# A three-layer graph kernel: the loads of the column numbers move from SyncE's DMA queue to ScalarE's

## The reference

```python
def _spmm(row, col, vals, x):
    msg = vals[:, None] * x[col]
    return jax.ops.segment_sum(msg, row, num_segments=N)

def _layer(x_prev, row, col, vals, W_a, b_a, W_b, b_b):
    h = _spmm(row, col, vals, x_prev)
    z = (h + x_prev) @ W_a.T + b_a + h * x_prev @ W_b.T + b_b
    return jnp.where(z >= 0, z, NEG_SLOPE * z)
```

## Time and profile before

| | |
|---|---|
| median of three runs | 11672.61 us (11668.24 to 11686.65) |
| the profiled execution | 11676.03 us |
| its span in the profile | 11674.3 us |
| TensorE busy | 9811.1 us (84%) |
| VectorE busy | 8287.8 us (71%) |
| ScalarE busy | 3867.5 us (33%) |
| three expansions, TensorE's first to last instruction of each | from 4527, 6908 and 9291 us, for 875, 872 and 877 us in the windows |
| DMA over the span | 1744.93 MB, mean 149 GB/s; in the expansions 335 to 337 GB/s |

### The profile page before, as it was taken

One profiled execution on the slowest core, in us unless ns is written; L12 is line 12 of the kernel. 1 busy time (PEld: TensorE's weight loads), 2 busy tenths in 40 slices (PEclk: granted clock), 3 DMA queues, 4 the chain that ended last, 5 costly groups with the idle time before them and its releaser, 6 DMA issues.

```text
span 11674.3 us, 234500 instructions
## 1 busy us (share of the span) xinstructions
PE 9811.1 (84%) x66108; PEld 8442.8 (72%) x66109; DVE 8287.8 (71%) x13757; ACT 3867.5 (33%) x12047; POOL 5876.3 (50%) x4395
## 2 busy tenths in 40 slices
PE   6898997689999947998888789988787899878877
PEld 4677776467777736997676679986666799867666
DVE  6877776777777746776666667766666677766666
ACT  0566665046666602662000036630000256400001
POOL 7577776047777710003777710027777300177774
PEclk8666666766666657999999999999999999999999
DMA  2111111011111194998666779986666799966666
GB/s 78 17 4 4 4 4 15 5 3 4 4 4 4 4 26 158 343 341 256 190 191 187 184 190 343 346 275 190 186 190 187 158 338 346 303 187 192 190 188 139
DMA packets 1150180, 1744.93 MB, mean 149 GB/s; under 512 B 472915, under 2 KB 524183, under 8 KB 1149494
## 3 DMA queue, kind: packets, MB, share of 16 engines
q0 software_dynamic: 430880, 809.77, 30.8%
q1 hardware_dynamic: 719254, 934.66, 27.1%
HBM read 990.83 MB, written 752.96 MB: 149 GB/s over the span
## 4 chain that ended last, share of the span: by engine, by line
DMA 24%; issue 17%; PE 15%; DVE 3%; POOL 2%; ACT 2%; POOLq 1%; SPq 0%; DVEq 0%; ACTq 0%
DMA messages<-work 13%; DMA work<-messages,work 11%; PE ps L885 6%; PE ps L876 6%; POOL work L499 2%; ACT work L658 2%; DVE work L1248 2%; PE ps L856 2%; PE ps L893 1%; PE ps L913 1%; PE ps L914 1%; POOLq L497 0%; PE ps L903 0%; SPq L576 0%; POOLq L493 0%
## 5 line engine op out<-in xcount | busy, mean ns | idle before, releaser
L499 POOL DMA_INDIRECT work<-messages,work x3000 | 3250.7, 1084 | 4194.6 <-issue 4022.7
L885 PE MATMUL ps<-work 128*128 128x125 f32 x24000 | 3394.6, 288 | 910.4 <-DVE work L1248 878.4
L885 PEld LDWEIGHTS ps<-work 128*128 128x128 f32 x24000 | 2911.5, 193 | 1393.5 <-DVE work L1248 1379.8
L475 POOL DMA_INDIRECT sorted_edges<-stage,run_idx x1270 | 2420.2, 1906 | 1456.4 <-DMA sorted_edges<-stage,run_idx 535.4
L1248 DVE SCALAR_TENSOR_TENSOR work<-work,iota_p 128x500 f32<-128x500 f32 x3000 | 2219.9, 740 | 1295.7 <-DMA work<-messages,work 1281.3
L876 PE MATMUL ps<-xb,work 125*128 x21504 | 2458.0, 276 | 149.7 <-DVE work L1220 83.0
L876 PEld LDWEIGHTS ps<-xb,work 125*128 125x128 f32 x21504 | 2423.7, 192 | 183.9 <-issue 183.5
L769 PEld LDWEIGHTS ps<-hT 128*128 128x128 f32 x12700 | 2187.4, 272 | 392.5 <-issue 371.4
L769 PE MATMUL ps<-hT 128*128 128x80 f32 x12700 | 2190.7, 357 | 286.6 <-ACT hT L617 217.7
L658 ACT ACTIVATE work<-ps,work 128x128 f32<-128x128 f32 x5376 | 1511.4, 371 | 1394.1 <-PE ps L876 730.7
L614 ACT ACTIVATE hT<-iota_p,place 128x128 f32<-128x128 f32 x4826 | 1437.2, 387 | 403.4 <-DVE place L1057 381.1
(11 more groups left out here) (199 smaller groups left out, 3843.1 us busy)
## 6 DMA issues: line engine op xcount, KB each, us to landing
messages<-work SPq DMA_DIRECT2D x2688, 256.0 KB, 6.2
work<-slot_cols SPq DMA_DIRECT2D x672, 256.0 KB, 6.0
work<-messages,work POOLq DMA_INDIRECT x3000, 3.8
sorted_edges<-stage,run_idx POOLq DMA_INDIRECT x1270, 3.2
out_x<-xb SPq DMA_DIRECT2D x150, 125.0 KB
work<-lane_places SPq DMA_DIRECT2D x508, 5.5 KB, 3.4
out_x<-xb SPq DMA_DIRECT2D x4, 1562.5 KB
sorted_edges<-hT SPq DMA_DIRECT2D x4, 906.0 KB
```

The costliest lines, as they stand in the source:

```text
L475: pool.indirect_dma_start(out=sorted_edges[p], out_offset=bass.IndirectOffsetOnAxis(ap=run_idx[:, q, k:k + 1], axis=0), in_=stage[:, q, k ...
L499: pool.indirect_dma_start(out=ck[:, n, :], out_offset=None, in_=messages, in_offset=bass.IndirectOffsetOnAxis(ap=idx[:, h * BU + n:h * BU ...
L885: last = t.matmul(part[n], ck[:, n, j * D:(j + 1) * D], sel[:, n % SELB, j, :], start=j == 0, stop=j == CH - 1)
```

## The change

SyncE no longer issues the loads of column numbers. ScalarE does: the first four of a layer ahead of its first body, and in each body one load after each of the messages 2, 6, 10 and 14, for the same buffer of the next body, after a wait for the four one-hots that read the buffer. ScalarE's bodies are written as first, middle and last, since the last body loads nothing; SyncE's are now all alike. The wait for `cols_stored` (the table is in HBM) moves along.

```diff
--- before.py
+++ after.py
@@ -562,27 +562,15 @@
             sp.dma_start(row_at, tile_rows.rearrange("p t -> (p t)")[0:TB].rearrange("(a t) -> a t", a=1)).then_inc(offsets_in, DMA)
             sp.dma_start(base_of, tile_base.rearrange("p t -> (p t)")[0:TB].rearrange("(a t) -> a t", a=1).to_broadcast([P, TB])).then_inc(offsets_in, DMA)
             sp.dma_start(messages[0:CHUNKS, CH * D:REC].rearrange("(p c) j -> p c j", p=DP), slot_row).then_inc(slots_stored, DMA)
-            sp.wait_ge(cols_stored, DMA)
-
-            cols_of = slot_cols.rearrange("(n c) -> n c", c=BATCH * GE)
             new_out = out.rearrange("(n h r) (l d) -> n l r h d", h=2, r=BLK, d=D)
             with sp.Fori(0, LAYERS) as la:
-                def load_cols(i, h):
-                    sp.dma_start(col_row[:, h, :], cols_of[bass.ds(i * CB + h, 1), :].to_broadcast([P, BATCH * GE])).then_inc(col_row_in[h], DMA)
-
-                def store_messages(i, last):
+                def store_messages(i):
                     for n in range(AU):
                         sp.wait_ge(msg_ready[n % 2], la * (GROUPS // 2) + i * (AU // 2) + (ACREDIT + n // 2 + 1))
                         sp.dma_start(messages[bass.ds(i * (AU * P) + n * P, P), 0:CH * D], msg[:, n % MR, :]).then_inc(msg_stored[n % MR], DMA)
-                        if n % BATCH == BATCH - 1 and not last:
-                            sp.wait_ge(col_hot_ready, la * GROUPS + i * AU + (n + 1))
-                            load_cols(i + 1, n // BATCH)
-
-                for h in range(CB):
-                    load_cols(0, h)
-                with sp.Fori(0, ABODIES - 1) as i:
-                    store_messages(i, False)
-                store_messages(ABODIES - 1, True)
+                with sp.Fori(0, ABODIES) as i:
+                    store_messages(i)
+
                 with sp.Fori(0, DSTEPS // DU) as i:
                     for k in range(DU):
                         sp.wait_ge(xb_ready, la * DSTEPS + i * DU + (k + 2))
@@ -638,6 +626,8 @@
                 s.activation(val_of.rearrange("p (t k j) -> p k j t", k=GPP, j=CH)[:, k, :, :],
                              ps[:, k, 0:CH * DP].rearrange("p (j t) -> p j t", j=CH), ACT.Copy).then_inc(vals_kept, 1)
             act.wait_ge(vals_kept, GPP)
+            act.wait_ge(cols_stored, DMA)
+            cols_of = slot_cols.rearrange("(n c) -> n c", c=BATCH * GE)
 
             with act.Fori(0, LAYERS) as la:
                 def free_message(eng, i, n, first):
@@ -647,7 +637,10 @@
                     elif not first:
                         eng.wait_ge(msg_stored[n % MR], la * (GROUPS // MR * DMA) + i * (AU // MR * DMA))
 
-                def keep_messages(i, first):
+                def load_cols(i, h):
+                    act.dma_start(col_row[:, h, :], cols_of[bass.ds(i * CB + h, 1), :].to_broadcast([P, BATCH * GE])).then_inc(col_row_in[h], DMA)
+
+                def keep_messages(i, first, last_body):
                     act.wait_ge(msg_ready[0], la * (GROUPS // 2) + i * (AU // 2) + ACREDIT)
                     s.activation(val_now, val_of[:, bass.ds(i * (AU * CH), AU * CH)], ACT.Copy).then_inc(val_now_ready, 1)
                     act.wait_ge(val_now_ready, la * ABODIES + i + 1)
@@ -658,10 +651,17 @@
                             last = s.activation(msg[:, n % MR, j * D:(j + 1) * D], ps[:, n % PR, j * D:(j + 1) * D], ACT.Copy,
                                                 scale=val_now[:, n * CH + j:n * CH + j + 1])
                         last.then_inc(msg_ready[0], 1)
-
-                keep_messages(0, True)
-                with act.Fori(1, ABODIES) as i:
-                    keep_messages(i, False)
+                        if n % BATCH == BATCH - 2 and not last_body:
+                            act.wait_ge(col_hot_ready, la * GROUPS + i * AU + (n + 2))
+                            load_cols(i + 1, n // BATCH)
+
+                for h in range(CB):
+                    load_cols(0, h)
+                keep_messages(0, True, False)
+                with act.Fori(1, ABODIES - 1) as i:
+                    keep_messages(i, False, False)
+                keep_messages(ABODIES - 1, False, True)
+                act.sem_inc(act_copies, 1)
 
                 with act.Fori(0, BBODIES // 2) as i:
                     for h in range(2):
```

## The result

The changed kernel takes 11777.77 us, median of 4 runs (11759.19 to 11782.69), beside 11679.63 us for the kernel before in the same comparison (11668.24 to 11694.44). The ratio is 1.008, 95% interval [1.0067, 1.0094]: slower by 98 us. The forecast was 11636 us, 37 us less than the 11672.61 us measured for the kernel before at that time. The profiled span is 11776.1 us, 101.8 us longer than before.

What follows compares the result with a forecast made beforehand. The prediction took DMA rate, through free message buffers and VectorE, to bound the expansions. From 11676.0 us it took 36 (transfers) and 2 (layer starts), then 3.4 for the median, and said 11636 us; range for 8 in 10: 11575 to 11725.

Steps and rivals of the forecast that it cites:

- what bounds the kernel: In the three expansions: DMA rate sets when message buffers are free, then VectorE's scaling, its one-hot and TensorE's gap.
- the gap between bodies: TensorE's idle time between expansion bodies, 0.77 us of 15.35 us each, set by how far VectorE is ahead.
- the issue on ScalarE: Four load issues a body, 0.36 us each, hidden in ScalarE's idle time: 0, at most 7 us slower.
- The start of a layer: First four loads go out about 1 us earlier at two of three layers: 2 us gained.
- the transfers: Loads in another queue overlap stores, recovering a quarter of their surplus: 0.22 us a body, 36 us gained.
- a load's surplus: A load's extra DMA time over a store, estimated at 0.94 less 0.724 us from the mixed and last-body windows.
- a worse mix: Rival side of the transfers: the 0.22 us added once more per load, 145 us slower; 0.05 with a late ScalarE.
- a late ScalarE: Rival: ScalarE issues of 1.5 us or more exceed its idle cover twice a body; 0.05 with a worse mix.
- that place is what goes away: On SyncE's queue, the load's place between store 3 and store 4 of its quartet disappears; no time was given.
- an inner rate over 350 GB/s: Sign that the forecast is right: DMA rate in the inner stretch of an expansion.
- The overtaking: Rival: loads in their own queue delay store 3 by 0.38 us a body, 63 us slower, 11736 us; chance 0.23.
- Its signs: For the overtaking: loads landing under 5 us, stores over 6.3 us, VectorE's store waits over 85 us in 700.

Runs made afterwards that it cites:

- e16: Kernel before with the loads of column numbers in the bodies left out; 11607.15 us, ratio 0.99, 117 us faster.
- e7: Kernel before, loads still on SyncE's queue but behind the stores of messages 1, 5, 9 and 13; 11817.35 us, ratio 1.0088.
- e10: Kernel before, loads still on SyncE's queue but behind the stores of messages 2, 6, 10 and 14; 11794.72 us, ratio 1.0084.
- e3: Kernel before with the loads issued by GpSimd in a queue of its own, once the four one-hots are made; 12240.75 us, ratio 1.0036.
- e9: Changed kernel with each ScalarE load held until odd message 3, 7, 11 or 15 is made; 11745.5 us, ratio 1.0049 to the kernel before.
- e13: Kernel before, on SyncE, only a body's first load moved, from behind store 3 to behind store 1; 11753.29 us, ratio 1.0025.
- e6: Changed kernel, unchanged, run again on another chip; 11833.98 us, ratio 1.01 to the kernel before.
- e5: Kernel before, unchanged, run again for a profile beside the other runs; 11698.63 us in a single run.
- e14: Kernel before, on SyncE, first load left behind store 3, the others moved behind stores 5, 9 and 13; 11732.66 us, ratio 1.0007.
- e1: Kernel before with TensorE's read of 16 offsets done once a layer instead of once a body; 12181.17 us, ratio 0.9992.
- e2: Changed kernel with TensorE's read of 16 offsets done once a layer; 12253.71 us, ratio 1.0047 to the kernel before.
- e4: Kernel before with TensorE's read of 16 offsets moved behind group 0, into the body's work; 13134.33 us, ratio 1.0773.
- e17: Kernel before, on SyncE, loads behind the stores of messages 1, 7, 11 and 13; 12263.65 us, ratio 1.0032.
- e18: Kernel before, on SyncE, loads behind the stores of messages 1, 5, 9 and 15; 12322.16 us, ratio 1.0075.

## Why the prediction was wrong

**Right: what bounds the kernel.** The expansions, the full DMA engines and the gap between bodies were the place: 97.5 of 101.8 us. e16 confirms that DMA rate and gap hang together and what lies in them.

**Right: the issue on ScalarE.** 0.34 us against 0.36 taken; ScalarE is no later for it, since it waits longer for TensorE than before. The start of a layer brought nothing measurable: outside the expansions the trace differs by 4 us, the other way.

**The step that failed: the transfers.** The prediction took a quarter of a load's surplus of 0.22 us over a store as recovered, -36 us. The term measured +97.5 us, 0.59 us for each of 165 bodies (worked out). It had named the other side, a worse mix at up to 145 us more, but gave it, together with a late ScalarE, a chance of 0.05. Two things stood in it without a price. The first is the place: "that place is what goes away" is said in the part on what the change removes, and no term follows. e7 and e10 lose 0.88% and 0.84% with one queue and with SyncE issuing everything, and in e7 the first load of a body ends 0.83 us behind the store ahead of it instead of 0.38, so what a load costs depends on the order around it. The second is the other queue, taken as a gain: e3, with the loads in their old order among the stores, loses 0.36%, and e9, with the loads back at about their old places, 0.49%. The change does both at once and loses 0.8 to 1.0%. Either alone costs, the place alone as much as the whole; how the loss of this kernel divides between them is not shown.

**A reading that was not quite right.** The earlier trace rows are called free of loads, but the last load was issued at 5377.9 us and landed at 5383.9 (worked out). A stretch behind it:

```profile
5384.00:5390.00 6.00, 6.00 (x56) 6.00 (x55) 4.39 (x10) 3.98 (x15) 0.00 (x0) 1.00 1.03 366
```

By 366 GB/s a load's surplus comes to 0.26 us instead of 0.22. That is not what failed.

**The test was misread in advance.** The prediction held that an inner rate over 350 GB/s would show it right. It came to 330 at a share of 1.04. A DMA share above 1 was read as engines that can't be slower, only better mixed; it says how long packets were under way, and packets can take longer.

**The rival that came nearest.** The overtaking was priced at 11736 us and put its finger on store 3 and the gap between bodies; the measured time is 42 us above it and outside the range. e10 fits its place: one step ahead of store 3, the whole loss. Its signs did not come, so its nearness in time says nothing for its mechanism. Loads of a queue of their own did not land in under 5 us but in 5.7, stores at 6.2 rather than over 6.3, and VectorE waits 67 us for stores, not over 85. By the rule of the Trainium skill (page "DMA: Bandwidth & Descriptors", section "Queues, rings and completion order") that queues take turns, the load should have been served ahead of some of the stores queued before it. The landing times, of the first engine or of the last, don't show that. And overtaking isn't needed: a single queue, with no second one to take turns with, loses as much. A load ahead of store 3 in every body, which the rival priced at 63 us, costs 29 us on one queue (e13). By the same page of the Trainium skill, section "Issuing engines are not separate DMA queues", the time would not have changed. Nothing was gained, as it says, but the measured time rose, and e3 loses 0.36% with the order kept.

**What stays open.** Why a load two places earlier is served slower. In the slow kernels fewer transfers are under way when the first load goes out: 5.8 to 6.8 in e6, e7 and e10 against 8.2 in e5 (worked out from issues and landings, as are the next figures). But e14 has 5.7 there as well. Its first load, though in its old place behind store 3, ends 0.84 us behind that store, as long as e10's does, and its lowest rate with the bodies laid over each other is 209 GB/s, near e10's 202; yet it loses only 8 us. A short queue thus goes with a slow first load, and neither decides the time. Why the first three loads together cost nearly three times their parts was not settled, nor why a second queue costs anything where the order is kept. What the longer read of the offsets adds is not known beyond e1 and e2; e14 shows that a read as long can cost next to nothing.

## What to carry to other kernels

Where DMA engines are full and a ring of buffers ties them to the compute engines, the position of a transfer in the order matters as well as its bytes: all four loads moved one or two stores ahead cost 0.8 to 0.9% on one queue, about four fifths of what leaving them out gains. A second queue cost 0.4% with the order kept. A full share says nothing of the rate; read the GB/s beside it, in slices finer than the loop body. Before moving transfers to another engine for the issue time, ask whether any engine waits for the issue; here none did, and nothing was gained. The places in the old queue are a change of one line, and can be tried first.

## What the hardware showed that was not expected

- The rate of the DMA engines falls around each load of one row to 128 partitions, from 390 to 400 GB/s between the dips to between 171 and 316, and in the slow order to 111, with the share at 0.97 to 1.00 in the deepest dips.
- The 16 engines finish one load of 256 KB 2.4 us apart when the queue is full; in e16, with the queue short, they finish a store within 0.4 us (worked out from the landing events).
- TensorE's read of 16 offsets takes 1.30 us at least and 1.62 in the median before the change, 2.11 after it (in the other runs the medians lie between 1.38 and 2.25), and 5.96 with the table read one entry further and behind a group's products (e4; which of the two makes it was not tried).
- Two tiny stores of 16 bytes a body cost 0.0005 and 0.0014 of the time, at most 0.0015 and 0.0023 by the intervals.
- The chips differ more than the kernels: 11680 to 12226 us for the kernel before, so only ratios on one chip could be used. The expansions hardly take part in it: 2630.5 us in e1 and 2622.9 in e5, while the rest takes 9556 and 9074 us. On the two slow chips (e1 to e4, e17, e18) TensorE's granted clock is 0.85 in the gathering, from 5500 to 6700 us, where e5 and e7 have 1.00; in the expansions it is full on both.
